# Moving GpSimd's scale and shift of x, splitting the masks anew, and halving the final softmax around three gelus

## The reference

```
h = relu(layernorm(x))
for l in 0, 1, 2:                          # x below starts as h
    scores = leaky(si[:, None] + sj[None, :] + b[l])      # si, sj: two dot products of each token
    attn = softmax(where(mask, scores, -inf), axis=-1)
    h = layernorm(x + attn @ x) * g1 + beta1
    x = layernorm(h + gelu(h @ W1) @ W2 + b2) * g2[l] + beta2[l]
x = x_input + x
h = relu(layernorm(x))                     # final stage
Wh = h @ W;  e = where(adj > 0, leaky(s_i + s_j), -9e15)
x = x + leaky(softmax(e, axis=1) @ Wh)     # softmax over the other axis
```

## Time and profile before

| what | value |
| --- | --- |
| median of 3 runs | 2215.66 us (2211.63 to 2218.41) |
| the profiled execution, its own time | 2218.18 us |
| its span | 2216.4 us |
| TensorE busy | 1932.6 us, 87% |
| VectorE busy | 1653.3 us, 75% |
| ScalarE busy | 1217.3 us, 55% |
| GpSimd busy | 920.8 us, 42% |
| TensorE's mean granted clock | 0.953 |
| DMA | 52.33 MB, mean 24 GB/s |

### The profile page before, as it was taken

How to read it: one execution, slowest core, us unless ns; L and a number is a source line. 1 busy time by engine, 2 the same in 40 slices (tenths; PEclk the granted TensorE clock), 3 DMA queues, 4 the chain that set the end, 5 groups by cost and what they waited for, 6 DMA issues and landing times. The chain is left out here.

```text
span 2216.4 us, 30835 instructions
## 1 busy us (share of the span) xinstructions
PE 1932.6 (87%) x11009; PEld 1638.5 (74%) x11009; DVE 1653.3 (75%) x4941; ACT 1217.3 (55%) x1924; POOL 920.8 (42%) x657
## 2 busy tenths in 40 slices
PE   3888889998899989989889989899889998898985
PEld 2677777777777867778778777777777777777874
DVE  6677786778877797777877778677886778777653
ACT  2555555556466555565555556555555555556552
POOL 2345443435343443434434344443443335343542
PEclk9999999999999999999999999999999999999997
DMA  4000100010000110001100000000100010000000
GB/s 152 20 29 20 58 10 11 10 39 29 10 20 1 39 39 1 20 1 44 34 1 20 20 26 33 0 20 20 48 11 20 1 39 30 10 10 1 30 1 19
DMA packets 40481, 52.33 MB, mean 24 GB/s; under 512 B 2910, under 2 KB 30856, under 8 KB 40328
## 3 DMA queue, kind: packets, MB, share of 16 engines
q1 hardware_dynamic: 40328, 50.37, 6.9%
HBM read 41.97 MB, written 8.39 MB: 23 GB/s over the span
## 5 line engine op out<-in xcount | busy, mean ns | idle before, releaser
L481 PE MATMUL acc<-w_hi,gelu_hi 128*128 128x256 f32 x1536 | 481.1, 313 | 6.6 <-DVE gelu_lo L947 6.6
L1229 POOL TENSOR_TENSOR gelu_lo<-g_full,gelu_hi 128x512 fp32r<-128x512 f32 x240 | 313.0, 1310 | 339.3 <-ACT gelu_hi L697 326.6
L481 PE MATMUL acc<-w_hi,gelu_lo 128*128 128x256 f32 x1536 | 441.8, 288 | 0.0
L481 PE MATMUL acc<-w_lo,gelu_hi 128*128 128x256 f32 x1536 | 441.5, 287 | 0.0
L689 ACT ACTIVATE g_full<-ps_u,vec_all 128x512 f32<-128x512 f32 x384 | 259.6, 688 | 326.6 <-PE ps_u L454 201.1
L415 PE MATMUL acc<-x_nat,probs 128*128 128x257 f32 x1536 | 385.0, 401 | 50.1 <-DVE normed L910 26.0
L415 PEld LDWEIGHTS acc<-x_nat,probs 128*128 128x128 f32 x1536 | 284.8, 195 | 147.8 <-ACT probs L664 49.1
L1198 POOL TENSOR_TENSOR columns<-columns 128x4 f32<-128x4 f32 x128 | 136.0, 1063 | 591.7 <-DVE columns L829 591.7
L481 PEld LDWEIGHTS acc<-w_hi,gelu_hi 128*128 128x128 f32 x1536 | 301.3, 196 | 13.2 <-DVE gelu_lo L947 9.2
L481 PEld LDWEIGHTS acc<-w_lo,gelu_hi 128*128 128x128 f32 x1536 | 302.3, 197 | 4.1
L481 PEld LDWEIGHTS acc<-w_hi,gelu_lo 128*128 128x128 f32 x1536 | 299.9, 195 | 0.0
(11 more groups left out here) (123 smaller groups left out, 3796.8 us busy)
## 6 DMA issues: line engine op xcount, KB each, us to landing
adj_in<-adj_dram SPq DMA_DIRECT2D x64, 256.0 KB, 2.7
x_nat<-x_dram SPq DMA_DIRECT2D x16, 512.0 KB, 5.1
x_res<-x_dram SPq DMA_DIRECT2D x16, 512.0 KB, 4.1
out_dram<-x_res SPq DMA_DIRECT2D x64, 128.0 KB, 1.7
x_res<-L_gnn_W_dram SPq DMA_DIRECT2D x5, 1024.0 KB, 5.3
probs<-L_gnn_W_dram SPq DMA_DIRECT2D x1, 1024.0 KB, 9.8
attn_row<-L_gnn_attn_w_dram SPq DMA_DIRECT2D x1, 768.0 KB
g_row<-L_gnn_g_dram SPq DMA_DIRECT2D x1, 384.0 KB
```

Source lines behind the costliest of these rows:

```text
L481: last = pe.matmul(acc[side][c // 2][:, cols:cols + D], h[:, r, tok], w[:, layer, f, :], start=False, stop=(f == FC - 1 and i == 2), skip_ ...
L1229: pool.tensor_tensor(gelu_lo[:, f % RING, :], g_full[:, f % 2, :], gelu_hi[:, f % RING, :].bitcast(F32), ALU.subtract).then_inc(lo_done[0] ...
```

## The change

It changes the order of work, and no arithmetic:

1. layer_input on GpSimd waits for two things more: the scale for a new semaphore, max_begun, which the first instruction of neighbour_max (L865) signals; the shift (or the addition to x_res) for the low part of gelu 3.
2. The masks: VectorE takes chunks 0 and 1, GpSimd 2 and 3.
3. final_exps is cut in two: chunks 0 and 1 stay ahead of gelu 0, chunks 2 and 3 go behind gelu 2, between the halves of ff_apply (L670). final_scale and TensorE's waits in final_out are halved to match.
4. VectorE's order: in slots 5 and 0 final_mask, the masks 0 and 1 of the next graph, or final_norm come before neighbour_max, and final_apply right behind it; gelu 3's low part always directly behind these; gelu 4's low part always behind bounded_scores; layer_scores in halves on both sides of h_rest.
5. residual_shift on GpSimd goes behind the inverse root of the input's normalization, ahead of gelu 5's low part.

```
@@ final_out (TensorE)
-                pe.wait_ge(wh_scaled.sem, wh_scaled.at(g))
                 for c in chunks:
+                    if c < 2 and step is not None:
+                        pe.wait_ge(ln2_apply.sem, ln2_apply.at(step, c + 1))
...
+                        if c == 0 and j % 2 == 0:
+                            pe.wait_ge(wh_scaled.sem, wh_scaled.at(g, j // 2 + 1))
@@ exps (ScalarE)
-                    act.wait_ge(q_masked[j % 2].sem, q_masked[j % 2].at(n, j // 2 + 1))
+                    part = q_masked[j // 2]
+                    act.wait_ge(part.sem, part.at(n, j % 2 + 1))
@@ pair_body (ScalarE)
                         ff_apply(n - 1, other, 0)
+                    if s.late is not None:
+                        final_exps(s.late[0], (2, 3))
+                    if not s.begins:
                         ff_apply(n - 1, other, 1)
...
-                        final_exps(s.final[0])
+                        final_exps(s.final[0], (0, 1))
@@ neighbour_max and bounded_scores (VectorE)
-                dve.tensor_scalar(s_j8[:, :], s_j, 1.0 - SLOPE, None, ALU.mult)
+                dve.tensor_scalar(s_j8[:, :], s_j, 1.0 - SLOPE, None, ALU.mult).then_inc(max_begun.sem, 1)
...
-                    if j >= 2 and j % 2 == 0:
+                    if j in (1, 2):
                         masked(j - 1)
-                masked(NC - 1)
@@ pair_body (VectorE)
+                    if s.final is not None and s.layer_a == 0:
+                        final_norm(*s.stats)
+                    if s.keep is not None and s.layer_a == 0:
+                        final_mask(*s.keep)
+                    if s.prepare is not None and s.side == 1:
+                        prepare_masks(s.prepare, 1, (0, 1))
                     neighbour_max(n + 1, other)
+                    if s.final is not None and s.layer_a == 0:
+                        final_apply(*s.final)
+                    gelu_rest(n, 3)
                     if s.late is not None:
                         final_leaky(s.late[0], free, (2, 3))
...
+                    bounded_scores(n + 1, other, s.late[0] if s.late is not None else None)
+                    gelu_rest(n, 4)
+                    if s.keep is not None and s.layer_a > 0:
                         final_mask(*s.keep)
@@ layer_input and mask_scores (GpSimd)
                 pool.wait_ge(ln2_apply.sem, ln2_apply.at(n))
+                if attention:
+                    pool.wait_ge(max_begun.sem, max_begun.at(n + 2))
...
+                if attention:
+                    pool.wait_ge(lo_done[1].sem, lo_done[1].at(n + 1, 2))
...
-                for j in range(0, NC, 2):
+                for j in range(NC // 2, NC):
@@ pair_body (GpSimd)
-                    if s.layer == LAST:
-                        residual_shift(pair, s.side)
                     if s.late is not None:
                         final_add(*s.late)
...
                     if s.prepare is not None:
                         inverse_root(ln0_chain, s.prepare, ln0_rstd, rstd_x)
+                    if s.layer == LAST:
+                        residual_shift(pair, s.side)
```

More of the change, by code:

```diff
@@ L550, in slot @@
                 if s.late is not None:
-                    pe.wait_ge(ln2_apply.sem, ln2_apply.at(n - 1))
-                    final_out(s.late[0], free, (0, 1))
+                    final_out(s.late[0], free, (0, 1), n - 1)
                 if not soon:
@@ L712, in final_low, with final_exps @@
                 act.activation(low_sb[:, :], banks[1][:, :], ACT.Copy, scale=SLOPE).then_inc(g_low.sem, 1)
-            def final_exps(g):
-                for j in range(NC):
+            def final_exps(g, chunks):
+                for j in chunks:
                     act.wait_ge(g_neg.sem, g_neg.at(g, j + 1))
@@ L771, in pair_body @@
                         final_low(s.ff_graph, free)
[L772 removed]
+                        final_exps(s.ff_graph, range(NC))
                         continue
@@ L803, in _ @@
             final_low(B - 1, acc[0])
-            final_exps(B - 1)
+            final_exps(B - 1, range(NC))
             output_low(B - 1, acc[0])
@@ L852, in input_shift, with token_dots @@
                                          op0=ALU.mult, op1=ALU.mult).then_inc(ln0_shift.sem, 1)
[L854 to L859, removed]
+            def token_dots(side, layer, chunks):
+                for c in chunks:
+                    for t, to in ((0, s_i), (1, s_j)):
+                        last = dve.tensor_tensor_reduce(junk[:, (2 * c + t) * D:(2 * c + t + 1) * D], x_nat[:, side, c, 0:D],
+                                                        attn_row[:, layer, t, :], 1.0,
+                                                        bias_col[:, 0, layer:layer + 1] if t == 0 else 0.0,
+                                                        ALU.mult, ALU.add, to[:, c:c + 1])
                 return last
@@ L962, in ff_norm @@
                 if late is not None:
-                    final_scale(late)
+                    final_scale(late, 0)
                 def half(b):
@@ L985, in ff_norm @@
                 half(1)
+                if late is not None:
+                    final_scale(late, 1)
                 if follows and scores is None:
@@ L1062, in final_bounded, with final_scale @@
                 negate(NC - 1)
-            def final_scale(g):
-                dve.wait_ge(g_exp.sem, g_exp.at(g))
-                dve.reciprocal(col_r[:, :], col_sum[:, :]).then_inc(g_r.sem, 1)
-                dve.wait_ge(g_r.sem, g_r.at(g))
-                for c in range(NC):
+            def final_scale(g, half):
+                chunks = (2 * half, 2 * half + 1)
+                cols = slice(2 * half, 2 * half + 2)
+                dve.wait_ge(g_exp.sem, g_exp.at(g, 2 * half + 2))
+                dve.reciprocal(col_r[:, cols], col_sum[:, cols]).then_inc(g_r.sem, 1)
+                dve.wait_ge(g_r.sem, g_r.at(g, half + 1))
+                for c in chunks:
                     last = dve.tensor_scalar(wh[:, c, 0:D], wh[:, c, 0:D], col_r[:, c:c + 1], None, ALU.mult)
@@ L1181, in pair_body @@
                         h_rest(n + 1, s.layer_a)
+                    if s.prepare is not None:
+                        layer_scores(n + 2, s.side, s.prepare, (1,))
             each_pair(pair_body)
             ff_norm(B * LAYERS - 1, 1, None, False)
-            final_scale(B - 2)
+            final_scale(B - 2, 0)
+            final_scale(B - 2, 1)
             final_leaky(B - 2, acc[0], range(NC))
@@ L1189, in _ @@
             final_bounded(B - 1, 1, acc[0])
-            final_scale(B - 1)
+            final_scale(B - 1, 0)
+            final_scale(B - 1, 1)
             final_leaky(B - 1, acc[0], range(NC))
```

59 lines of the change are left out of this document (23 added, 36 removed).

## The result

The changed kernel takes 2273.61 us (median of 4 runs, 2270.20 to 2274.47) against 2216.70 us (median of 4) of the kernel before beside it. The ratio is 1.0263, with a 95% interval of 1.0240 to 1.0286: slower, by 57 us where 39 were forecast, and inside the range. The profiled execution took 2273.11 us, its span is 2271.3 us and its mean granted clock 0.940.

What follows compares the result with a forecast made beforehand. TensorE was taken as the bound, busy for 87% of the span, with 284 us not busy and low-clock stretches to win. Terms of +10.5, +8, +5.6, +1, +15 and -1 made +39 on 2215.66: 2255 us, range 2198 to 2284.

Steps and rivals of the forecast that it cites:

- The masks: Slots 1, 2, 3: fourth exponential ends 6.9 us after the first score starts (t), 1.9 later; 1.3 without meeting gelu 4.
- The late slots, front and chain: Slots 1 and 3: TensorE restarts earlier, but scores start only -0.2 and +0.8 us; with the masks +1.7 and +2.7.
- the 1 us named as a sign of being wrong: The prediction is wrong if scores of slots 1 and 3 start over 1 us earlier within the slot.
- Slots 2 and 0: final_apply runs unheld, 1.4 us in slot 2; slot 2 +0.3 us with the masks, slot 0 -3.2 us (attend_out earlier).
- Slot 5: TensorE gets bound rows after 5 us idle, residual_shift holds input_shift for 2.3 us: +0.8 us (bounds 0, +1.5).
- Slot 4: Down 4 waits for gelu 4's low part, attend_out starts at 1314.3 against 1313.1: +1.0 us (bounds +0.4, +1.5).
- The clock at attend_out: Gaps before the fourth exponential in slots 1, 2, 3 lower TensorE's clock: 0.7 us (bounds 0, 1.7), 21 slots, +15.
- (a): Rival: the gain in front survives in slots 1 and 3, scores 3.4 and 2.3 us earlier: 2196 us; chance 0.20.
- (b): Rival: the masks cost 1.3 us and the clock nothing: 2212 us, no change that shows; chance 0.15.
- (c): Rival: the clock falls at every late fourth exponential, costing 1.7 us, with 1.0 in slots 4 and 5: 2291; chance 0.16.
- (d): Rival: a ScalarE table switch costs 1.4 us beyond its load, two more in 14 late slots: 2294 us; chance 0.03.

Runs made afterwards that it cites:

- experiment 1: The changed kernel with the masks split as before (VectorE chunks 1 and 3, GpSimd 0 and 2): 2198.91 us, ratio 0.9925.
- experiment 4: The kernel before with the new split of the masks alone, gelu 4's low part staying ahead of the scores: 2252.12 us, ratio 1.0163.
- Experiment 3: The changed kernel without GpSimd's new waits for max_begun and gelu 3 in slots 1 and 3: 2227.69 us, ratio 1.0043.
- the seventh: The changed kernel with the old split of the masks and without GpSimd's new waits in slots 1 and 3: 2177.54 us, ratio 0.9815.
- experiments 8 and 9: 8: the seventh, gelu 4's low part early, slot 5's mask work behind the scores, 2167.53 us; 9: that, all final exponentials ahead of gelu 0, 2185.21 us.
- experiment 5: The changed kernel with all four final exponentials ahead of gelu 0 again, final_scale still in halves: 2283.44 us, ratio 1.0288.

## Why the prediction was right, and where its sizes were off

**The masks: right.** The fourth exponential ends at t+6.6 (forecast 6.9, from t+5.05), in three runs made of 1.1 for the split and 0.45 for the meeting with gelu 4. That this decides the sign is shown by experiment 1, and by experiment 4 on the other kernel.

**The late slots, front and chain: right, and its size nearly.** TensorE's gap went to 1.32 us (1.4 forecast), and little of it reached the scores: in the slot they start 0.9 us earlier in slot 1 (0.2 forecast) and 0.1 later in slot 3 (0.8 later forecast). That is close to the 1 us named as a sign of being wrong, and over it, by 0.2 at most, in four of the seven slots 1, since the kernel before starts them 27.4 to 28.9 us into the slot and the changed one 27.7 in all but one. The first o_tmp came 1.25 us earlier in slot 1, where at most 1 was named, and 0.3 in slot 3. final_add stands behind the shift and low_row behind output_low. Experiment 3 shows that GpSimd's new waits make this loss. One part was wrong: behind the short gap the clock was 0.62 to 0.63 over some 4.5 us in eight of the 14 late slots, six of them slots 1, where it was to be kept.

**Slots 2 and 0: right in kind.** final_apply takes 1.38 us. Slot 0 gave 2.3 instead of 3.2: TensorE still waited 1.91 us for the columns there, and the clock was 0.69 over 5.5 us behind it, which the term did not hold. Slot 2 came out at 0.0 instead of +1.0, for the clock stayed full in this pair (in two of the seven it was 0.69).

**Slot 5: the mechanism right, its size wrong.** The hole is there (6.03 us, 5 forecast) and residual_shift holds input_shift for 2.30 us, as forecast. The slot lost 3.3 instead of 0.8 us. attend_out ended 1.9 us later than before, not 0.8; TensorE ran at 0.52 over 4.2 us behind the hole. The rest came behind it: VectorE's normalization of the attention (L936) was held by gelu 7's low part on GpSimd (2.33 us for four instead of 1.38), so that TensorE's turn came in two pieces, 0.83 us apart. The prediction stopped at attend_out and did not look at what a later attend_out meets next. 2.5 us in seven slots make 17 us that the sum lacked.

**Slot 4: wrong in sign.** attend_out starts 1.3 us later, as forecast, behind a gap of 2.41 us for gelu 4's low part. But at the attention's final turn, behind a gap of 2.22 us, the clock held: its 8 transposes take 1.32 us, where they took 1.67 before, behind a gap of 2.42 (0.63 over the next 2.2 us then, 1.00 now). The low stretch now lies at attend_out, behind the gap for gelu 4's low part: 0.78 over its first 5.5 us. It ended only 1.2 us later than before. The slot is 0.5 us shorter.

**The clock at attend_out: the term that was mis-sized.** I took 0.7 us in each of 21 slots, +15. It is 2.1 to 2.6 us in slots 1 and 3, in all seven pairs, and nothing in five of the seven slots 2, 1.7 in two: 14 x 2.3 = 32, and 36 with slot 2. The upper bound of 1.7 was too low too, since the stretches from which I took it were shorter than the 8.4 us here. Without the clock the two slots cost less than I worked out: +0.8 and +1.5 against +1.7 and +2.7, by an earlier score in slot 1 and the meeting with gelu 4. So the steps miss by +17 (clock), -15 (slots 1 and 3), +17 (slot 5), -12 (slot 4), +6 (slot 0) and -2 (slot 2), +11 in all. The other 7 of the 18 us are not taken apart here; they lie in the pairs that lost more than the one that I read (one lost 12.8 us), in the first pair and in the last. The direction was right by its mechanism. That the sum came near was luck in part: errors of both signs met, up to 17 us each.

**The rivals.** (a), the gain in front survives: not in the changed kernel, but in the seventh, where masks and chain are out of its way: from gelu 0's cast in slot 0 to the one in slot 4 it takes 173.9 us, the kernel before 181.7 and the changed kernel 185.7. That stretch holds the gains of slots 0 and 2 as well; of the front itself 2.1 and 1.1 us reach the scores of slots 1 and 3 there (26.5 us into the slot), not the 3.4 and 2.3 of (a), and the halving is worth 18 us in 14 slots (experiments 8 and 9). (b) fell with the first experiment. (c) is right for slots 1 and 3 and wrong for slot 2. (d) fell: after the change the load takes 1.28 us and the next instruction of ScalarE starts within 0.02 us of its end.

**What stays open.** Why the clock falls at one gap and not at another of the same length. It decides a good part of what the halving is worth: without it (experiment 5) attend_out kept its clock in half of the late slots, which is 18 of the 30 us that it was expected to cost. The gap of 1.32 us behind the final exponentials was followed by a low clock in 6 of 7 slots 1 and in 2 of 7 slots 3 of the changed kernel, in 5 of the 14 of experiment 1 and of experiment 3, in 4 of the eighth kernel and in 1 of the seventh. No run here changes only the place of a gap.

## What to carry to other kernels

Where two engines share a row of chunks and the consumer needs the last of them, deal the chunks out in turns: the third and fourth chunk in the hands of the slower engine made the fourth 1.5 us late, and that alone turned a gain of 0.75% (experiment 1) into a loss of 2.6%. A wait put into an engine's queue to keep it off another engine is paid by all that stands behind it: look for the slots in which a chain passes through that queue (final_add here) and leave the wait out there. And two delays in front of one TensorE operation can't be priced one by one and added: here they shared a loss of clock of 36 us, of which either edit alone took away 28 or 29.

## What the hardware showed that I had not expected

A low clock came with gaps in pieces, none of them over 1.6 us. Behind idle times of 1.56, 0.49, 0.32 and 0.34 us, with 2.6 us of work between, the granted clock over the next 5.5 us was 0.53 to 0.62, 14 times of 14. It had fallen already in the third piece, whose two records take 1.22 us instead of 0.70; the last gap is short for that reason. With 0.34 us in front instead of 1.56 it was 1.00 in most slots and 0.69 in some. But the length of the front gap doesn't decide it: behind 2.00, 0.49, 0.31 and 0.86 us (experiment 5) the clock was 1.00 in 7 of 14 late slots.

A single gap of 1.32 us was followed by a granted clock of 0.62 over 4.5 us, the mean of a stretch at the lower level and one at the higher, or by 1.00, with the same work behind it; one of 2.96 us, in the kernel before, by 0.50 to 0.68 in each of its 14 late slots; one of 6.03 us by 0.52.

An instruction of VectorE on 4 columns takes as long as GpSimd's work on a 128 x 1024 tile lasts: 2.30 us for L858, 2.19 for L885. GpSimd's side pays as well: its two masks take 3.10 us together where VectorE's gelu 4 meets them, and 2.85 or 2.86 where it doesn't.
